# A decoder layer's self-attention: values and probabilities kept as two 2-byte parts, and two bias rows loaded at another place

## The reference, cut to what matters

```python
x = x + self_attention(layernorm(x))            # the part that the change touches
x = x + cross_attention(layernorm(x), ctx_1024, mask)
x = x + mixture_of_4_experts(layernorm(x))      # first layer with b1, gelu, second layer with b2

# self_attention(hidden), hidden is [2048, 256]:
norm   = ||hidden|| per row
scaled = hidden / (norm + 1e-9)
q = scaled @ Wq.T + bq
v = scaled @ Wv.T + bv
scores = q @ (q @ A).T / 16
out = softmax(scores) @ v * norm
```

## Time and profile before

| | |
|---|---|
| median of 3 runs | 823.52 us (822.39 to 825.96) |
| time of the profiled execution | 824.94 us |
| its span, first to last instruction | 823.0 us, 19881 instructions |
| PE busy | 760.4 us (92%) |
| PE weight loads busy (overlap PE) | 686.0 us (83%) |
| DVE busy | 629.1 us (76%) |
| ACT busy | 457.3 us (56%) |
| POOL busy | 165.5 us (20%) |
| mean granted clock of PE | 0.977 of full |

### The profile page before, as it was taken

The page is one execution under the profiler, slowest core; times in us unless marked ns, Lnnn a source line. Parts: engine busy times, 40 slices in busy tenths (PEclk is TensorE's granted clock), DMA queues, the critical chain, the costliest instruction groups (busy, mean ns, idle before and its releaser), DMA issues. The chain is left out here.

```text
span 823.0 us, 19881 instructions
## 1 busy us (share of the span) xinstructions
PE 760.4 (92%) x6226; PEld 686.0 (83%) x6227; DVE 629.1 (76%) x1608; ACT 457.3 (56%) x930; POOL 165.5 (20%) x254
## 2 busy tenths in 40 slices
PE   3878889999999999999999999999997768999996
PEld 2768779899898898988988889899895657999996
DVE  4983746797898888888889888888886754777773
ACT  2554536666766667666666666666664612444342
POOL 3100121212303123031230312303212011222221
PEclk9999989999999999999999999999999959999999
DMA  6233233213233131231312314213189290111110
GB/s 218 72 106 108 64 131 121 102 33 109 61 112 106 38 111 62 97 106 38 123 61 85 106 38 131 76 62 106 39 288 368 88 335 27 37 41 39 39 33 15
DMA packets 51146, 80.94 MB, mean 98 GB/s; under 512 B 4894, under 2 KB 29216, under 8 KB 50976
## 3 DMA queue, kind: packets, MB, share of 16 engines
q1 hardware_dynamic: 49232, 75.63, 27.2%
q0 software_dynamic: 1872, 4.76, 1.6%
HBM read 45.60 MB, written 35.18 MB: 98 GB/s over the span
## 5 line engine op out<-in xcount | busy, mean ns | idle before, releaser
L1135 ACT ACTIVATE ps_cross<-flip 128x512 f16<-128x512 f32 (+1 forms) x256 | 124.8, 515 | 110.4 <-PE flip L847 89.3
L1360 DVE TENSOR_TENSOR ps_cross<-flip,ps_cross 128x512 f16<-128x512 f32 (+1 forms) x256 | 145.0, 584 | 29.4 <-ACT ps_cross L1135 28.5
L1321 ACT ACTIVATE exp_cross<-exp_cross,xneg 128x1024 f32<-128x1024 f32 (+1 forms) x128 | 122.7, 960 | 28.0 <-DVE xneg L1520 28.0
L847 PE MATMUL flip<-ident,exp_cross 128*128 128x128 f32 (+1 forms) x832 | 130.9, 280 | 6.7 <-DVE ps_cross L1360 3.6
L836 PE MATMUL scores<-keys_cross,qt 128*128 128x402 f32 x512 | 126.8, 369 | 4.9 <-DVE xneg L1520 3.1
L847 PEld LDWEIGHTS flip<-ident,exp_cross 128*128 128x128 f32 (+1 forms) x832 | 95.2, 142 | 14.2 <-DVE ps_cross L1360 5.1
L724 PE MATMUL scores<-keys_self,u_tile 128*128 128x512 f32 x384 | 102.2, 403 | 4.3 <-issue 2.4
L823 PE MATMUL flip<-vals_self,ps_self 128*128 128x256 f32 x768 | 104.1, 290 | 0.0
L858 PE MATMUL cross_out<-vals_cross,ps_cross 128*128 128x128 f16 (+1 forms) x832 | 100.6, 222 | 0.2 <-DVE ps_cross L1360 0.2
L823 PEld LDWEIGHTS flip<-vals_self,ps_self 128*128 128x128 f32 x768 | 97.2, 195 | 0.0
L860 PE MATMUL cross_out<-vals_cross,ps_cross 128*128 128x64 f16 (+1 forms) x832 | 94.0, 194 | 0.0
(11 more groups left out here) (199 smaller groups left out, 1210.4 us busy)
## 6 DMA issues: line engine op xcount, KB each, us to landing
rows_dram<-pads SPq DMA_DIRECT2D x17, 520.0 KB, 4.0
w_piece<-W SPq DMA_DIRECT2D x32, 256.0 KB, 2.9
w_dram<-w_high SPq DMA_DIRECT2D x32, 256.0 KB, 2.3
w_dram<-w_piece SPq DMA_DIRECT2D x32, 256.0 KB, 2.7
w1s<-w_dram SPq DMA_DIRECT2D x8, 1024.0 KB, 12.4
w2s<-w_dram SPq DMA_DIRECT2D x8, 1024.0 KB, 12.5
u_dram<-u_out SPq DMA_DIRECT2D x4, 1024.0 KB, 5.9
u_tile<-u_dram SPq DMA_DIRECT2D x16, 256.0 KB, 2.7
```

Source lines behind the costliest of these rows:

```text
L847: tr = pe.transpose(flip[0:rows, bank(use), n * P:(n + 1) * P], exp_cross[:, h % 2, m * P:m * P + rows], ident[:, :])
L1135: return act.activation(out, in_, ACT.Copy, **kw)
L1321: act.activation(exp_cross[:, h % 2, cols], exp_cross[:, h % 2, cols], ACT.Exp, bias=xneg[:, h % 2, 1:2], scale=-1.0, accum_out=xden[:, ha ...
L1360: return dve.tensor_tensor(out, full, hi, ALU.subtract)
```

## The change

The values of the self attention and its probabilities become f16 parts, 2 bytes each, instead of fp32r. The probabilities, at most 1, are scaled by 16384 (`P_TOP`) as they are split; the values are scaled by a factor `self_scale` that keeps them within 16384 (`SELF_TOP`); both factors are taken out again through `norms`, by one more instruction at the end of the prologue. The factor comes from a bound on the values: the square root of the sum of all squares of Wv, plus the largest magnitude of the bias. The squares are summed along each partition by DVE, over the partitions by a matmul with a matrix of ones, the root is a power on POOL. ACT's and DVE's splitting of the values takes the factor from memory; that of the probabilities has it as an immediate. `ps_self` has four slots now and `self_hi` of group 3 no longer waits for group 0. `exp_self` and `ps_self` move to the memory that the smaller values leave free, and `b1_row` and `b2_row` get memory of their own, so that they are loaded right after the first weight piece, ahead of the loop. Declarations of semaphores and of `self_scale` are left out of the diff.

```diff
@@ -42,6 +42,8 @@
 V_TOP = 4096.0
+SELF_TOP = 16384.0
+P_TOP = 16384.0
 XHALF = 2 * 512
@@ -128,8 +131,6 @@
     w2s = sb("w2s", [P, E * WE], F32R, ffn)
-    b1_row = sb("b1_row", [P, E * DF], F32, ffn)
-    b2_row = sb("b2_row", [P, E * D], F32, ffn)
     rows = sb("rows", [P, RING, REC], F32, ffn)
@@ -145,7 +146,9 @@
     keys_self = sb("keys_self", [P, 2, C, N], F32R, keep)
-    vals_self = sb("vals_self", [P, T, 2, D], F32R, keep)
+    vals_self = sb("vals_self", [P, T, 2, D], F16, keep)
+    exp_self = sb("exp_self", [P, N], F32, keep)
+    ps_self = sb("ps_self", [P, 4, 2, 512], F16, keep)
 
@@ -160,6 +163,8 @@
     v_tmp = sb("v_tmp", [P, 2, D], F32, pro)
+    v_bound = sb("v_bound", [P, 6], F32, pro)
+    bound16 = sb("bound16", [P, 1], BF16, pro)
     stats_pro = sb("stats_pro", [P, T, 6], F32, pro)
@@ -192,8 +197,6 @@
     x_tile = sb("x_tile", [P, D], F32, loop)
-    exp_self = sb("exp_self", [P, N], F32, loop)
-    ps_self = sb("ps_self", [P, 3, 2, 512], F32R, loop)
     w_piece = sb("w_piece", [P, 2, 512], F32R, loop)
@@ -236,6 +239,8 @@
     dest_i = sb("dest_i", [P, 1], U32, loop)
+    b1_row = sb("b1_row", [P, E * DF], F32, loop)
+    b2_row = sb("b2_row", [P, E * D], F32, loop)
     loop.close()
@@ -498,6 +507,8 @@
         load_piece(0)
+        sp.dma_start(b1_row[:, :], bass.AP(io["b1"].tensor, 0, [[0, P], [1, E * DF]])).then_inc(b_loaded, 16)
+        sp.dma_start(b2_row[:, :], bass.AP(io["b2"].tensor, 0, [[0, P], [1, E * D]])).then_inc(b_loaded, 16)
         sp.wait_ge(padding_set, 4)
@@ -547,8 +558,6 @@
         load_w1(3)
-        sp.dma_start(b1_row[:, :], bass.AP(io["b1"].tensor, 0, [[0, P], [1, E * DF]])).then_inc(b_loaded, 16)
-        sp.dma_start(b2_row[:, :], bass.AP(io["b2"].tensor, 0, [[0, P], [1, E * D]])).then_inc(b_loaded, 16)
         sp.wait_ge(cross_scores_ready, 8 * T)
@@ -614,6 +623,9 @@
         for g in range(4):
+            if g == 2:
+                pool.wait_ge(bound_step, 3)
+                pool.tensor_tensor(v_bound[:, 2:3], v_bound[:, 1:2], plus_half[:, 0:1], ALU.pow).then_inc(bound_rooted, 1)
             cols = slice(4 * g, 4 * g + 4)
@@ -732,6 +744,8 @@
                     pe.wait_ge(u_lo_ready, C * (g - 1) + o + 1)
+                if g == 0 and o == 1:
+                    pe.wait_ge(bound_step, 3)
                 out = self_out if o == 0 else cross_out
@@ -759,6 +773,9 @@
                       lambda b, c: xt_pro[:, g % 2, b, c, :]).then_inc(pro_q_ready, 1)
+            if g == 0:
+                pe.wait_ge(bound_step, 2)
+                pe.matmul(cross_out[:, 0:1], ones[:, :], bound16[:, :], start=True, stop=True).then_inc(bound_summed, 1)
             if g < GROUPS - 1:
@@ -820,7 +837,7 @@
                 for a, b in ((0, 0), (0, 1), (1, 0)):
-                    mm = pe.matmul(self_out[:, 0:D], ps_self[:, g % 3, a, n * P:(n + 1) * P], vals_self[:, m, b, :],
+                    mm = pe.matmul(self_out[:, 0:D], ps_self[:, g, a, n * P:(n + 1) * P], vals_self[:, m, b, :],
                                    start=(m == 0 and a == 0 and b == 0), stop=(m == T - 1 and a == 1))
@@ -1166,7 +1183,9 @@
                 act.wait_ge(pro_v_biased, 4 * g + n + 1)
-                copy(vals_self[:, 4 * g + n, 0, :], v_tmp[:, n % 2, :]).then_inc(pro_v_hi, 1)
+                act.wait_ge(self_scale_step, 2)
+                act.activation(vals_self[:, 4 * g + n, 0, :], v_tmp[:, n % 2, :], ACT.Copy,
+                               scale=self_scale[:, 0:1]).then_inc(pro_v_hi, 1)
             u_hi(g)
@@ -1219,11 +1238,9 @@
             act.wait_ge(self_flipped, 4 * j + g + 1)
-            if g == 3:
-                act.wait_ge(self_p_used, 4 * j + 1)
-            elif k >= 1:
-                act.wait_ge(self_p_used, 4 * j if g == 0 else 4 * j + g - 3)
-            copy(ps_self[:, g % 3, 0, :], flip[:, bank(("s", g)), :]).then_inc(self_p_hi, 1)
+            if k >= 1:
+                act.wait_ge(self_p_used, 4 * j + g - 3)
+            copy(ps_self[:, g, 0, :], flip[:, bank(("s", g)), :], scale=P_TOP).then_inc(self_p_hi, 1)
 
@@ -1409,7 +1426,12 @@
                 xt_lo_pro(0)
+                dve.tensor_tensor_reduce(v_tmp[:, :, :].rearrange("p c n -> p (c n)"), w_raw[:, 1, :, :].rearrange("p c n -> p (c n)"),
+                                         w_raw[:, 1, :, :].rearrange("p c n -> p (c n)"), 1.0, 0.0, ALU.mult, ALU.add,
+                                         v_bound[:, 0:1]).then_inc(bound_step, 1)
                 statistics_pro(1)
+                dve.wait_ge(bound_step, 1)
+                dve.tensor_scalar(bound16[:, :], v_bound[:, 0:1], 1.02, None, ALU.mult).then_inc(bound_step, 1)
         scale_rows(1)
@@ -1419,10 +1441,24 @@
                                          op1=ALU.subtract).then_inc(pro_q_lo, 1)
+            if g == 0:
+                dve.wait_ge(bound_summed, 1)
+                dve.tensor_copy(v_bound[:, 1:2], cross_out[:, 0:1]).then_inc(bound_step, 1)
             if g < GROUPS - 1:
...
                 statistics_pro(g + 2)
+            if g == 0:
+                dve.tensor_reduce(v_bound[:, 3:4], bv_row[:, :], AX.X, ALU.max, apply_absolute_value=True).then_inc(bound_step, 1)
+                dve.wait_ge(bound_step, 4)
+                dve.wait_ge(bound_rooted, 1)
+                dve.tensor_tensor(v_bound[:, 4:5], v_bound[:, 2:3], v_bound[:, 3:4], ALU.add).then_inc(bound_step, 1)
+                dve.wait_ge(bound_step, 5)
+                dve.tensor_scalar(v_bound[:, 5:6], v_bound[:, 4:5], 1e-30, 1.0 / SELF_TOP, ALU.max, ALU.mult).then_inc(bound_step, 1)
+                dve.wait_ge(bound_step, 6)
+                dve.reciprocal(self_scale[:, 0:1], v_bound[:, 5:6]).then_inc(self_scale_step, 1)
+                dve.tensor_scalar(self_scale[:, 1:2], v_bound[:, 5:6], 1.0 / P_TOP, None, ALU.mult).then_inc(self_scale_step, 1)
+                dve.wait_ge(self_scale_step, 2)
             for n in range(4):
@@ -1435,8 +1471,9 @@
                         dve.wait_ge(pro_v_biased, 4 * g + m + 1)
-                        low(vals_self[:, 4 * g + m, 1, :], v_tmp[:, m % 2, :],
-                            vals_self[:, 4 * g + m, 0, :].bitcast(F32)).then_inc(pro_v_lo, 1)
+                        dve.scalar_tensor_tensor(out=vals_self[:, 4 * g + m, 1, :], in0=v_tmp[:, m % 2, :], scalar=self_scale[:, 0:1],
+                                                 in1=vals_self[:, 4 * g + m, 0, :], op0=ALU.mult,
+                                                 op1=ALU.subtract).then_inc(pro_v_lo, 1)
             if g < GROUPS - 2:
@@ -1485,6 +1522,9 @@
                                                  op1=ALU.subtract).then_inc(cross_v_lo, 1)
+        dve.wait_ge(norm_step, 16)
+        dve.tensor_scalar(norms[:, :], norms[:, :], self_scale[:, 1:2], None, ALU.mult).then_inc(norm_step, 1)
+        dve.wait_ge(norm_step, 17)
         dve.wait_ge(cross_v_lo, MC)
@@ -1500,7 +1540,8 @@
             dve.wait_ge(self_p_hi, 4 * j + g + 1)
-            low(ps_self[:, g % 3, 1, :], flip[:, bank(("s", g)), :], ps_self[:, g % 3, 0, :].bitcast(F32)).then_inc(self_p_lo, 1)
+            dve.scalar_tensor_tensor(out=ps_self[:, g, 1, :], in0=flip[:, bank(("s", g)), :], scalar=P_TOP,
+                                     in1=ps_self[:, g, 0, :], op0=ALU.mult, op1=ALU.subtract).then_inc(self_p_lo, 1)
 
```

More of the change, by code:

```diff
@@ L109, in emit @@
     v_scale = sb("v_scale", [P, 2], F32)
+    self_scale = sb("self_scale", [P, 2], F32)
     bg_row = sb("bg_row", [P, E], F32)
@@ L261, in emit @@
     pro_v_hi = sem("pro_v_hi")
+    bound_step = sem("bound_step")
+    bound_summed = sem("bound_summed")
+    bound_rooted = sem("bound_rooted")
+    self_scale_step = sem("self_scale_step")
     pro_v_lo = sem("pro_v_lo")
```

## The result

The changed kernel takes 826.0 us, median of 20 runs (822.21 to 830.06), against 822.68 for the kernel before on the same chip (20 runs, 821.25 to 825.96): a ratio of 1.0032, 95% interval 1.0020 to 1.0043. By that ratio it is slower by 2.6 us, 0.3% (the medians differ by 3.3), and its median lies outside the range of the prediction. The profiled execution took 828.12 us, with a span of 826.3.

What follows compares the result with a forecast made beforehand. PE was taken to bound the loop and DVE the prologue. Terms of -5.9 (matmuls), +2.9 (prologue), -1.0 (bias rows leaving) and 0 (arriving) sum to -4.0 us, from 823.52 to 819.5 us; range 816.4 to 824.0.

Steps and rivals of the forecast that it cites:

- two-byte values and probabilities, loop and split: Loop and prologue: faster f16 value matmuls give -5.9 us, splitting the probabilities nothing, splitting the values costs 0.8.
- bound and norms on DVE: Prologue, DVE's queue: sum of squares +0.7 us, copy +0.1, bias reduction and small instructions +1.1, scaling of norms +0.2.
- bias rows moved to tile 0: Bias-row loads: -1.0 us where they leave the queue after w1s, 0 where they arrive behind the first weight piece.
- 36 of 48 on the path: Loop: value matmuls of groups 1 to 3 count, group 0's do not; 9.8 ns each, 0.35 us a tile.
- 0.6 + 0.35: Value matmuls: 0.6 us saved in tile 0, where all 48 count, and 0.35 us for a later tile.
- the last rival: Loop: PE's time is that of its weight loads, 97.2 us falling to 69.3, giving 797.5 us; chance 0.02.
- The split of the values: Prologue: factor from memory slows ACT's and DVE's parts, +0.2 us a pair; groups 0 and 1 pay 0.8.
- The bias rows, where they arrive: Ahead of the loop, behind the first weight piece: the delayed `u` tile is hidden, 0 us; up to 7 if ahead.
- the rival that used it: Tile 0: bias rows collide with the first weight piece, up to +7 us, 826.5 us; chance 0.05.
- The bias rows, where they leave: Behind the loop: POOL's last scatter no longer stands behind the rows' transfers, -1.0 us, bounds 0 and 2.58.
- Value matmuls, low part and idle time below 2 us: Signs: 24 value matmuls in about 2.65 us, `ps_self` low part not over 700 ns, idle after last scatter below 2 us.
- The sign of being wrong named for `w_high` of tile 0: Tile 0: ACT's `w_high` later than its barrier by more than before would show the prediction wrong.

Runs made afterwards that it cites:

- the bound elsewhere: Changed kernel, bias rows at their old place, bound moved to DVE's idle times, ACT and POOL: 819.29 us, ratio 0.9934; with unread transposes in TensorE's idle times 813.89 us, 0.9885.
- TensorE kept busy: Unread transposes added in TensorE's idle times of the prologue and behind the loop: kernel before 819.35 us, ratio 0.9950; changed kernel 822.48 us, 0.9975.
- one wait: Changed kernel, with SP issuing the bias rows only when POOL's four stores of pads have landed: 823.36 us, ratio 0.9992, against 1.0032 without it.

## Why the prediction was wrong

The runs split the change into three steps, in two chains: the kernel before, the bound elsewhere with the rows at their old place, the bound on DVE, the change; once as they are and once with the transposes. Each number is the difference of two ratios times 823 us, and good to 1.6 to 2.7 us by the intervals of the two (the sums to 0.9 and 2.1):

| step | predicted | as it is | TensorE kept busy |
|---|---|---|---|
| two-byte values and probabilities, loop and split | -5.9 + 0.8 = -5.1 | -5.4 | -5.4 |
| bound and norms on DVE | 0.7 + 0.1 + 1.1 + 0.2 = +2.1 | +4.4 | +3.1 |
| bias rows moved to tile 0 | -1.0 + 0 = -1.0 | +3.7 | +4.3 |
| sum | -4.0 | +2.6 | +2.1 |

**The matmuls: right.** 110.0 ns, and 0.30 us a tile in the changed kernel, 0.36 in the five with the bound elsewhere, as 36 of 48 on the path make it. Tiles 0 and 1 gained about 1 us where the rows stay away (41.22 and 41.73 to 40.25 and 40.70), as 0.6 + 0.35 had it; with TensorE kept busy, 39.27 against 38.21 and 40.54 decides nothing. The first twelve matmuls of tile 0 in the changed kernel, against 2.91 us in the earlier trace rows:

```profile
113.05 2.77 PE L840 MATMUL flip<-vals_self,ps_self 128*128 128x256 f16 x12
```

That is 12 ns less for each, not 26. They took twice as long as later ones in both kernels because the granted clock was 0.50 there (1.2 GHz, from 106.81 to 109.70 us before and from 113.05 to 115.60 after), and not because nothing overlaps, as the prediction read it. The weight loads lost 23.4 us of busy time at L840 and the time did not follow them, so the last rival is out. The Trainium skill, page "Perfetto Trace Analysis", section "Identifying the Most-Contended Engine", names the busy share of weight loads, beside the share of peak arithmetic, as the measure of TensorE's headroom; here the loads were no measure of what could be gained. The split of the values cost 0.5 to 1.2 us in the prologue (88.67 and 87.25, against 87.5 and 86.76 before), predicted 0.8.

**The bias rows, where they arrive: the step that failed.** "Moved past: the `u` tile of iteration 1, then the pieces' stores." That names the consumers on SP's own queue, and prices the `u` tile. It leaves out POOL's four stores, the first issued half a microsecond before the rows on another queue, and POOL's low part, which came late with them; and the pieces' stores were named but not followed to the load that waits for them. The failing sentence is "I take 0"; in its place the runs show +3.7 and +4.3 us for the move as a whole, and 3.3 back for one wait. A price of up to +7 stood there, and the rival that used it got 0.05 and 826.5 us, close to what was measured, though it had the first piece in mind, so the nearness is luck. The first piece was hit by 1 us at most in the mean: `w_high` starts 5.6 to 6.9 us after the barrier in the five profiles with rows ahead of POOL's stores, 5.26 and 6.02 in the two of the kernel before (5.70 with the transposes). Those five have 41.7 to 45.2 us from barrier to x1 of tile 1, four two-byte kernels with the rows behind w1s 38.2 to 40.7.

**The bias rows, where they leave: mis-sized.** Predicted -1.0 of the 2.58 us in the earlier trace rows. The changed kernel, timelines of POOL and of DVE:

```profile
632.43 0.40 POOL L655 COPY record<-x_old 128x256 f32<-128x256 f32 x1 [4.82 <-issue]
```

```profile
635.20 1.00 DVE L1561 CUSTOM_DVE_ANT_0 exp_cross<-scores,mask_bias 128x804 f32<-128x804 f32 x1 [1.36 <-POOL mask_bias L666]
```

This looks like the predicted gain, 2.58 to 1.36. It isn't the rows: the kernel before with TensorE kept busy has its rows behind w1s and 1.58, the run with the rows in tile 1 has 1.98. From scatter to copy it takes 6.1 to 7.1 us in seven profiles with the rows there and 5.8 to 6.7 in nine without. With TensorE kept busy it is 6.12 to 6.17 and 5.80 to 5.89: 0.3 us. But for 0.3 us the scatter is as late without the rows as with them, the bound of 0 that the step named.

**The bound: list right, its side effect not priced.** DVE's prologue in the changed kernel:

```profile
15.46 0.68 DVE L1429 CUSTOM_DVE_ANT_0 v_tmp<-w_raw 128x512 f32<-128x512 f32 x1
...
24.04 0.15 DVE L1446 COPY v_bound<-cross_out 128x1 f32<-128x1 f32 x1
24.64 0.69 DVE L1377 TENSOR_TENSOR xt_pro<-flip,xt_pro 128x512 fp32r<-128x512 f32 x1 [0.46 <-ACT xt_pro L1152]
...
28.02 0.41 DVE L1452 TENSOR_REDUCE v_bound<-bv_row 128x1 f32<-128x256 f32 x1
28.47 0.16 DVE L1455 TENSOR_TENSOR v_bound<-v_bound 128x1 f32<-128x1 f32 x1
...
28.93 0.13 DVE L1460 TENSOR_SCALAR self_scale<-v_bound 128x1 f32<-128x1 f32 x1
29.10 0.76 DVE L1468 TENSOR_TENSOR v_tmp<-scores,bv_row 128x256 f32<-128x256 f32 x2
30.11 0.89 DVE L1474 SCALAR_TENSOR_TENSOR vals_self<-v_tmp,self_scale,vals_self 128x256 f16<-128x256 f32 x2 [0.25 <-ACT vals_self L1187]
```

Against the same instructions before, the delay grows by 0.61 at the sum of squares (0.7 predicted), 1.07 at reduction and chain (1.1), 0.44 for the two pairs of each of groups 0 and 1 (0.4), and nearly nothing in groups 2 and 3, whose idle times shrink as predicted. But at the copy, predicted at 0.1, it grows by 0.7, and between the last `ctx_t` and `v_max` by 1.2 more. TensorE tells why; the changed kernel, and then the run with the bound on DVE and the idle time filled:

```profile
19.87 0.18 PE L778 MATMUL cross_out<-bound,ones 128*128 128x1 bf16 x1
22.86 1.97 PE L762 MATMUL flip<-ident,x_all 128*128 128x128 f32 x8 [2.81 <-DVE x_all L1404]
```

```profile
19.79 2.60 PE L781 MATMUL flip<-ident 128*128 128x128 f32 x22
22.76 1.09 PE L762 MATMUL flip<-ident,x_all 128*128 128x128 f32 x8 [0.38 <-DVE x_all L1436]
```

The eight transposes ahead of `xt_pro` took 1.10 us before, at full clock behind 1.31 us of idle time, and 1.97 here, at half clock from 22.0 us on, behind 2.81. DVE's added list made TensorE's idle time longer. From the first weight split to the first biased value it took 17.35 us before, 19.09 with the idle time filled, and 19.14 to 20.16 in three runs with a half-clock stretch there: 1.7 us of list, and up to 1.1 of clock. With TensorE kept busy bound and norms cost 1.7 us up to the barrier. That leaves 1.4 of the 3.1 us timed, 1.0 of them in the loop, without a cause that any run shows; 1.4 is within the noise of that step. The 1.2 us ahead of `v_max` are the clock as well: this way takes 9.3 us in the eight profiles without a half-clock stretch on it, 10.7 in the kernel before with 3.41 us of it, 11.9 here with 6.83. And much of it belongs to one execution. Four profiles of kernels with this same prologue and no transposes have 92.27, 91.48, 90.25 and 89.06 us from the first weight split to the barrier, with 17.07, 10.24, 10.24 and 6.83 us at half clock in it.

**What would show it.** Value matmuls, low part and idle time below 2 us came as listed, and the last of these for another reason than the one given. The first score matmuls of tile 0 were 5.2 us late, not 2.7: 0.5 by a later first load, 1.9 by the clock, the rest, 2.8, by the list, as forecast. Counted from the first weight split, the run with the rows behind POOL's stores has them only 1.5 us late. The sign of being wrong named for `w_high` of tile 0 hardly came: 0.7 us later in the mean.

**The 3.2 us behind the loop.** In the profiled execution the stretch from 641.63 us took 29.27 us, with half-clock stretches of 3.41 us from 643.23 and 6.83 from 656.88. Other executions of kernels with the same end took 26.5 to 27.7, the kernel before 26.03 and 26.54, and each kernel with TensorE kept busy 24.6 to 25.0. It goes with the clock, and most of it belongs to that one execution; timed, filling the idle times gave 4.0 to 5.3 us to four pairs of kernels, 4.1 to the one before and 4.7 to the changed one.

## What to carry to other kernels

A transfer that is moved has to be priced against every queue that is issued near its new place, and each of those transfers followed to what waits for it, two steps on; the first name on the same queue is not enough. An addition to the bounding engine of a stage can cost more than its instructions where it lets TensorE stand idle. And a difference between two profiled executions has to be seen with the part held still (here by filling TensorE's idle time), or in several profiles, before it is called the change's.

The best version joins the two-byte values with the bound outside DVE's busy stretch, the bias rows behind w1s, and unread transposes in TensorE's idle times: 813.89 us.

## What the runs showed of the hardware

- A transfer with large packets holds up another queue's small ones. In the changed kernel the row load of 2 MB has 128 packets of 16,384 bytes, 0.76 us each, POOL's stores 128 of 4,160 bytes, 0.16 us each. Without the rows beside them these stores land in a median of 3.6 us, beside them in 9.1. Eight of either on each of 16 engines in turn make 8 x 0.92 = 7.4 us (an estimate from these numbers). The Trainium skill, page "DMA: Bandwidth & Descriptors", section "Queues, rings and completion order", says that an engine takes turns between queues packet by packet; the trace agrees, in that the stores' packets lie between 104.59 and 115.26 us, spread over the rows' own. The section counts several descriptors to a packet; whether a packet of the trace is the same thing, no run shows.
- POOL's next large instruction behind its own stores comes late when they do: it starts 1.3 to 2.7 us after their last packet in the five profiles with the rows ahead of them, 4.6 to 6.1 in the eleven others, and no semaphore is named for it. A copy of 0.20 us (L671) starts right behind the issue, so POOL does not stop altogether. Two runs show that the instruction comes early again once the rows wait for the stores; what in POOL holds it, no run shows.
- Transposes that nobody reads, 10 or 22 at each of three places in the prologue and 4 to 18 at nine behind the loop, gave 0.5 to 0.6% in four pairs of kernels, and the granted clock between the records of tiles 14 and 15 was 1.00 (2.4 GHz) in each of them; 24 of them placed behind a wait instead of ahead of it cost 2.5 us.
